# Layer 3's flow attention: flows in four column strips and kept as rows of nodes, queries and values scaled as rows, sums of keys times values folded with Wo

## The chip, the cores and the metric

One core of a Trainium2 chip. The metric is the device time of one execution of the whole program, in microseconds (us), as a median over runs. Everything is float32 unless a row says otherwise.

## The reference, cut to what matters

The program runs four layers of a graph network on 625 nodes with 512 features. The last layer's mixer is a "flow attention" with 8 heads of 64 features, and only that is changed:

```
q = sigmoid(x @ Wq + bq)   k = sigmoid(x @ Wk + bk)   v = x @ Wv + bv      # per head h: 625 x 64
sink_incoming    = 1 / ((q + EPS) . (k.sum(nodes) + EPS))
source_outgoing  = 1 / ((k + EPS) . (q.sum(nodes) + EPS))
conserved_sink   = (q + EPS) . ((k * source_outgoing).sum(nodes) + EPS)
conserved_source = clip((k + EPS) . ((q * sink_incoming).sum(nodes) + EPS), -1, 1)
sink_allocation    = sigmoid(conserved_sink)
source_competition = softmax(conserved_source over nodes) * 625
kv = k.T @ (v * source_competition)                                        # 64 x 64 per head
o  = (q * sink_incoming) @ kv * sink_allocation
x  = x + o @ Wo + bo
```

Beside it stands the layer's graph term, `agg @ weight.T`, which is added to the residual x. After it come a layer norm, a small GELU network, another norm and a ternary network.

## The kernel before, in words

`layer3` is one block. The order on each engine is written out by hand, and engines meet at semaphores. TensorE fills eight PSUM banks: four in turn for ScalarE (`for_act`, freed by `scalar_freed`) and four in turn for VectorE (`for_dve`, freed by `vector_freed`). An entry n waits until entry n-4 of the same four has been freed. `kept(name)` waits until ScalarE has taken the named entry. A product of float32 is written once in the code and stands in the trace as two MATMUL records, each as long as its number of moving columns; a transpose (`turned`) is one record.

Nodes come as 5 tiles of 125 rows (TILES, ROWS), features as 4 chunks of 128 (CH), and where nodes are columns, they are cut into halves of 313 and 312 (HALVES). The order before is:

1. Queries, then keys, as features by nodes (`T[0]`, `T[1]`, 128 x 4 x 625): 16 entries of four products for ScalarE, which applies the sigmoid and sums over nodes into `part`.
2. `size`, then the values as rows of nodes (`("v", t)`: 5 tiles, four products of 512 columns each). VectorE adds the bias (L4337), and rounds the ternary network's weights in `weights_rounded` (L4300 to L4302).
3. `flows(0)`: both incoming flows of all 8 heads, into 16 rows of PSUM, for two halves. Its stationary operand `wide` has 16 columns and its eight products a half are issued one after the other. VectorE keeps them as 16 x 625 (`keep_flows`) and takes the reciprocal (L4340).
4. `spreads(0, i, ...)` multiplies the 16 x 625 reciprocals by a 0/1 matrix, so that each head's row is copied to its 64 features; VectorE multiplies queries and keys by them and sums over nodes (L4344). Then `flows(1)` with the new sums.
5. ScalarE does sigmoid and exp on 16 x 625; `spreads(1, ...)` spreads both results, and VectorE scales queries (L4357) and keys (L4369) with them.
6. The scaled keys are transposed into rows (`("key", t)`, ScalarE keeps them in `z`), `shift` folds a bias, `("kv", p)` makes four 128 x 128 products over nodes, `("out", p, a)` multiplies queries by the two heads' diagonal blocks, and ScalarE keeps the result.
7. `("wo", t)`: 5 tiles, four products of 512 columns each, after which the norm begins.

The five products of the graph term (`graph(t)`) are placed between these. ScalarE keeps them in `G`, and one VectorE addition puts them into x (L4375).

Layer 2 of the same program already computes attention scores in four column strips (L2344) and gathers them into rows with a small 0/1 matrix (`a_gather`); this part is not changed.

Of the kernel before, what the change touches and what calls it, by code (L numbers as in the profile page):

```python
# [6 lines left out]
ALU = mybir.AluOpType  # L7
# [4 lines left out]
BF16 = mybir.dt.bfloat16  # L12
# [3851 lines left out]
def layer3(core, c, d, out):  # L3864
# [9 lines left out]
    with ExitStack() as ctx:  # L3874
# [15 lines left out]
        junk = sb("junk", [128, 2 * CH, 313], BF16)  # L3890
        wide = sb("wide", [128, 2, CH * HW])
        spread = sb("spread", [128, 2, CH, 128])
        flow_rows = sb("flow", [128, NODES])
        keep_rows = sb("keep", [128, NODES])
        flow, keep = flow_rows[0:HW, :], keep_rows[0:HW, :]
        offset = sb("offset", [HW, 2])
        es = sb("es", [HW, 1])
        kv = sb("kv", [128, CH, 128])
        part = sb("part", [128, 2, 2, CH, 2])
        total = sb("total", [128, 2, CH])  # L3900
# [12 lines left out]
        oT, x2T, r2, R, xq = xaT, aggT, V, z, G  # L3913
# [10 lines left out]
            "widened", "inverse_made", "flows_kept", "clipped", "exponents_done", "sink_made", "source_made",  # L3924
            "queries_scaled", "keys_scaled", "kv_made", "attended", "rows_rounded", "hidden_rounded", "tile_done",
            "stored", "gains_folded"]}
# [7 lines left out]
        with nc.Block() as block:  # L3934

            @block.gpsimd
            def _(gp):
                nc.gpsimd.memset(wide[:, :, :], 0.0)
                nc.gpsimd.memset(back[:, :], -ROUND)
                nc.gpsimd.memset(spread[:, :, :, :], 0.0)  # L3940
                nc.gpsimd.memset(flow_rows[:, :], 0.0)
                nc.gpsimd.memset(keep_rows[:, :], 0.0)
                for i in range(2):
                    nc.gpsimd.memset(T[i][:, :, NODES:NODES + 1], EPS)
                nc.gpsimd.memset(kv[:, :, :], 0.0).then_inc(sem["cleared"], 1)
                gp.wait_ge(sem["cleared"], 1)
                for i in range(2):
                    for p in range(CH):
                        for k in range(2):
                            row = HEADS * i + 2 * p + k  # L3950
                            last = nc.gpsimd.tensor_copy(spread[0:HW, i, p, HDIM * k:HDIM * (k + 1)],
                                                         c.ident[0:HW, row:row + 1].to_broadcast([HW, HDIM]))
                last.then_inc(sem["cleared"], 1)
# [8 lines left out]
            def _(pe):  # L3962
# [43 lines left out]

                def flows(n):

                    pe.wait_ge(sem["widened"], n + 1)
# [4 lines left out]
                def spreads(n, i, src):  # L4014
                    for p in range(CH):
                        for a, b in HALVES:
                            for_dve(("spread", n, i, p, a), [product(128, [(spread[:, i, p, :], src[:, a:b])], b - a)])

                def graph(t):
                    for_act(("graph", t), [product(ROWS, [(aggT[:, k, rows_of(t)], W["g"][:, k, :]) for k in range(CH)],  # L4020
                                                   DIM)])
# [18 lines left out]
                pe.wait_ge(sem["wv_landed"], 16)  # L4040
                for t in range(TILES):
                    for_dve(("v", t), [product(ROWS, [(xaT[:, k, rows_of(t)], W["v"][:, k, :]) for k in range(CH)], DIM)])
# [577 lines left out]
```

## Time and profile before

| | |
|---|---|
| median of 3 runs | 1624.69 us (1623.59 to 1641.59) |
| the profiled execution: own time | 1628.42 us |
| its span, first to last instruction | 1626.7 us |
| from the first `size` product to the first `wo` product | 1485.59 to 1568.97 us of the span |
| from there to the end | 57.73 us |
| mean granted TensorE clock | 0.974 |

The trace lists each instruction with its start and length. Lengths of matmuls include the time for the result to come out, so consecutive ones overlap: what a block of products takes is the distance from its start to the start of the next block. PE is TensorE's matmul unit, PEld its loading of the stationary operand, DVE VectorE, ACT ScalarE, POOL GpSimd.

### The profile page before, as it was taken

What the parts mean: (1) busy time and instruction counts of PE and PEld (TensorE: products, weight loads), DVE (VectorE), ACT (ScalarE), POOL (GpSimd) and SP (SyncE); (2) the same over time, 40 slices, a digit from 0 to 9 for tenths busy, and PEclk for the clock granted to TensorE, in tenths of its full rate; (3) what the DMA queues carried; (4) which work ended last, traced back from release to release, by engine and by line L of the source; (5) the groups of instructions that cost most, each with busy time, mean ns of one, the idle gap of its engine ahead of it and who ended that gap; (6) DMA issues with size and microseconds to landing.
All of it is one profiled execution on the core that took longest, in us unless ns stands there. A gap on an engine that the chain in (4) does not pass through costs nothing. (4 is left out here: it accounts for less than half of the span.)

```text
span 1626.7 us, 25993 instructions
## 1 busy us (share of the span) xinstructions
PE 1546.7 (95%) x9350; PEld 982.2 (60%) x9351; DVE 877.8 (54%) x2376; ACT 497.8 (31%) x1178; POOL 112.0 (7%) x194
## 2 busy tenths in 40 slices
PE   6999999999899989998999999999999999999995
PEld 3687644664456589995476754665544444465453
DVE  7676767873366675623634435643633343441457
ACT  2462244430120132321556314621122232221124
POOL 1010000000000003441000000000000000110000
PEclk9999999999899899998999999999899999999997
DMA  5340363100441188960200031304789999550001
GB/s 177 96 132 15 116 213 136 39 8 0 174 170 38 41 311 274 302 200 29 73 26 26 1 116 46 102 0 207 304 352 425 428 428 399 228 175 1 1 0 32
DMA packets 58548, 237.57 MB, mean 146 GB/s; under 512 B 13022, under 2 KB 16729, under 8 KB 49498
## 3 DMA queue, kind: packets, MB, share of 16 engines
q1 hardware_dynamic: 45076, 209.69, 34.4%
q0 software_dynamic: 13376, 26.60, 5.6%
q8 instruction: 61, 1.00, 0.2%
q14 instruction: 35, 0.29, 0.1%
HBM read 225.99 MB, written 10.24 MB: 145 GB/s over the span
## 5 line engine op out<-in xcount | busy, mean ns | idle before, releaser
L105 PE MATMUL psum<-ahead_arena 125*125 125x257 f32 (+2 forms) x720 | 215.8, 457 | 1.1 <-issue 0.7
L105 PEld LDWEIGHTS psum<-ahead_arena 125*125 125x125 f32 (+1 forms) x720 | 130.5, 188 | 76.5 <-issue 63.6
L3246 PE MATMUL psum<-ahead_arena,ahead_W 128*32 128x512 f32 x928 | 107.1, 601 | 1.8 <-DVE ahead_W L3768 1.0
L3225 PE MATMUL psum<-ahead_arena,ahead_W 128*32 128x256 f32 x1856 | 106.4, 381 | 2.1 <-DMA ahead_arena<-in_L_ffn_W 1.7
L105 PE MATMUL psum<-a_W,1_xn_turned 128*125 128x512 f32 x200 | 89.4, 596 | 1.2 <-DVE a_u L1577 1.2
L799 DVE TENSOR_SCALAR a0e_ring<-a0e_node,a0e_key 125x640 bf16<-125x640 f16 x216 | 69.1, 384 | 33.7 <-PE psum L607 31.8
L3225 PEld LDWEIGHTS psum<-ahead_arena,ahead_W 128*32 128x32 f32 x1856 | 57.7, 110 | 41.8 <-issue 5.5
L607 PEld LDWEIGHTS psum<-a0e_tables,a0e_ring 125*125 125x125 bf16 x1080 | 67.5, 138 | 11.5 <-issue 9.5
L607 PE MATMUL psum<-a0e_tables,a0e_ring 125*125 x1080 | 72.0, 223 | 1.8 <-issue 0.9
L105 PE MATMUL psum<-a_W,a0l_H 128*125 128x512 f32 x168 | 72.7, 593 | 0.7 <-issue 0.7
L105 PE MATMUL psum<-e_hT,e_W 128*128 128x156 f32 x512 | 70.9, 297 | 0.0
L3752 DVE TENSOR_TENSOR ahead_W<-psum,ahead_W 128x256 f32<-128x256 f32 x58 | 21.9, 419 | 88.6 <-PE psum L3234 88.6
L105 PE MATMUL psum<-e_xgT,e_W 128*128 128x156 f32 x512 | 69.2, 296 | 0.0
L105 PEld LDWEIGHTS psum<-e_hT,e_W 128*128 128x128 f32 x512 | 68.4, 190 | 0.0
L105 PEld LDWEIGHTS psum<-e_xgT,e_W 128*128 128x128 f32 x512 | 68.3, 190 | 0.0
L3246 PEld LDWEIGHTS psum<-ahead_arena,ahead_W 128*32 128x32 f32 x928 | 29.9, 111 | 62.3 <-issue 53.2
L105 PEld LDWEIGHTS psum<-a_W,1_xn_turned 128*125 128x125 f32 x200 | 36.5, 188 | 44.2 <-issue 43.4
L105 PEld LDWEIGHTS psum<-a_W,a0l_H 128*125 128x125 f32 x168 | 31.4, 188 | 40.7 <-issue 40.7
L105 PE MATMUL psum<-1_xn_turned,a_qkv 128*128 128x313 f32 (+1 forms) x176 | 49.3, 435 | 0.8 <-ACT 1_xn_turned L1096 0.8
L3434 ACT ACTIVATE ahead_W<-psum 128x512 f32<-128x512 f32 x29 | 17.4, 598 | 92.8 <-PE psum L3246 85.1
L105 PE MATMUL psum<-1_edges_from_to,1_xn_rows 125*128 125x313 f32 (+1 forms) x160 | 43.0, 426 | 1.3 <-PEq L3112 1.3
L2206 POOL DMA_INDIRECT e_got<-expert_rows,e_at_i x30 | 39.5, 1318 | 60.9 <-DMA expert_rows<-e_rows 53.5
(829 smaller groups left out, 2690.4 us busy)
## 6 DMA issues: line engine op xcount, KB each, us to landing
ahead_arena<-in_L_ffn_W SPq DMA_DIRECT2D x52, 2048.0 KB, 13.5
e_W<-in_L_ffn_W SPq DMA_DIRECT2D x16, 2048.0 KB
1_xn_turned<-half_shares SPq DMA_DIRECT2D x16, 256.0 KB, 8.2
a_stage<-in_L_gnn_W SPq DMA_DIRECT2D x8, 512.0 KB, 8.1
ahead_arena<-in_L_gnn_W SPq DMA_DIRECT2D x2, 2048.0 KB, 10.6
a_W<-in_L_gnn_W SPq DMA_DIRECT2D x3, 1024.0 KB, 5.5
a_qkv<-half_shares SPq DMA_DIRECT2D x11, 256.0 KB, 3.3
a_W<-in_L_ffn_w_down POOLq DMA_DIRECT2D x1, 2816.0 KB, 15.7
```

What stands on the lines that cost most here:

```text
L105: last = nc.tensor.matmul(bank[0:rows, at:at + cols], lhs, rhs, start=(n == 0), stop=(n == len(terms) - 1))
L607: last = nc.tensor.matmul(sums[k % 2][0:ROWS, 128 * s:128 * (s + 1)], ring[:, b, rows_of(s)], targets, start=False, stop=False, skip_group ...
L799: nc.vector.tensor_scalar(ring[:, b, :], node[:, :], key[:, k, b:b + STARTS][:, bass.ds(tile, 1)], None, ALU.is_equal).then_inc(made[b], QUAD)
L2206: nc.gpsimd.indirect_dma_start(out=got[:, e % 2, t, :], out_offset=None, in_=c.expert_rows[0:(e + 1) * TOP1, :], in_offset=bass.IndirectOf ...
L3225: last = nc.tensor.matmul(hid[a][g * SL:(g + 1) * SL, 0:HC], xgT[:, k, :], Wa[b][a][:, k, g, :], start=(k == 0), stop=(k == CH - 1))
L3246: last = nc.tensor.matmul(sums[g * SL:(g + 1) * SL, :], hT[:, a, m, g * SL:(g + 1) * SL], Wb[b][a][:, m, g, :], start=(a == 0 and m == 0), ...
L3434: nc.scalar.activation(part, sums[:, :], ACT.Copy).then_inc(sem["parts_kept"], 1)
L3752: nc.vector.tensor_tensor(hT[:, a, :, :].rearrange("p c (g n) -> p (c g) n", g=QT), turn[a][:, 0:HC].rearrange("p (f n) -> p f n", n=SL), ...
```

## The change

- **Flows in strips.** `wide` becomes [128, 8, 32]: one 32-column stationary operand for each of 4 chunks of keys' sums and of queries' sums. The eight products of a half go to four column strips of the array, each strip with its own chunk, and its own 32 rows of PSUM. The four strips are added when they are turned into rows: `gather` (128 x 16) has a one for each head in each strip, and `row_flows` multiplies each tile of `strips` by it, giving 125 x 16 for a tile of nodes.
- **Rows of nodes.** Sigmoid outputs are also transposed to rows, queries (`("rows", 0, t)`) between the key products, keys (`("rows", 1, t)`) after the first value tile. VectorE copies them (`keep_rows`). Reciprocals, sigmoid and exp are now taken on 125 x 5 x 16 or 125 x 5 x 8 elements.
- **Sums over nodes by TensorE.** `node_sums` multiplies the reciprocals (stationary, 32 columns) by the rows of queries and keys, in four strips; ScalarE copies the bank, `("sums")` turns it back to features, `widen` builds the new `wide`. No flow is spread over features any more.
- **Scaling rows.** VectorE multiplies the rows of queries by the product of sink_allocation and sink_incoming, and the rows of values by the exponentials, with a per-head factor that is broadcast over 64 features. The queries are transposed back (`("back", t)`), keys are not scaled at all. The softmax's sum comes from a product with ones (`norms`) and is folded into `kv`.
- **Folding with Wo.** `M = kv.T-block @ Wo` (four products of 512 columns) replaces `out`; `wo` multiplies the transposed queries by `M`.
- The graph products go to VectorE's banks, and VectorE adds each of them to x; `shift` and the folding of `W1` come earlier. `spread`, `junk`, `flow` and `keep` are gone; GpSimd fills `own_head`, `gather`, `gather_sums` and `inverse` at the start of the block instead.

The core of the diff (waits and declarations largely left out):

```diff
-                    for a, b in FLOW_HALVES:
-                        for_dve(("flow", n, a), [product(HW, [(wide[:, i, HW * p:HW * (p + 1)], T[i][:, p, a:b])
-                                                              for i in range(2) for p in range(CH)], b - a)])
+                    for a, b in FLOW_HALVES:
+                        m = for_vector.add(("flow", n, a))
+                        pe.wait_ge(sem["vector_freed"], m - 3)
+                        for i in range(2):
+                            for p in range(CH):
+                                last = nc.tensor.matmul(for_vector.bank(m)[STRIP * p:STRIP * (p + 1), 0:b - a],
+                                                        wide[:, CH * i + p, :], T[i][:, p, a:b], start=(i == 0),
+                                                        stop=(i == 1))
+                        last.then_inc(sem["vector_filled"], 1)
+                def row_flows(n):
+                    pe.wait_ge(sem["vector_freed"], for_vector.nth(("flow", n, FLOW_HALVES[1][0])))
+                    for_dve(("rows_flow", n), [product(ROWS, [(strips[:, rows_of(t)], gather[:, :])], HW, at=HW * t)
+                                               for t in range(TILES)])
+                def node_sums():
...
+                    for turn in range(3):
+                        for i in range(2):
+                            for part_, tiles in enumerate([(0, 1, 2), (3, 4)]):
+                                if turn < len(tiles):
+                                    at, t = STRIP * (2 * i + part_), tiles[turn]
+                                    last = nc.tensor.matmul(for_scalar.bank(n)[at:at + STRIP, 0:DIM], inverse[:, t, :],
+                                                            R[i][:, t, :], start=(turn == 0), stop=(turn == len(tiles) - 1))
...
+                        if i and m < CH - 1:
+                            kept(("q", CH - 1, HALVES[1][0]))
+                            turn_rows(0, range(2 * m, min(2 * m + 2, TILES)))
...
-                for t in range(TILES):
-                    for_dve(("v", t), ...)
-                flows(0)
-                graph(0)
-                graph(1)
-                pe.wait_ge(sem["inverse_made"], 1)
-                for i in range(2):
-                    spreads(0, i, flow_rows)
-                graph(2)
-                flows(1)
-                graph(3)
-                spreads(1, 0, keep_rows)
-                graph(4)
-                spreads(1, 1, flow_rows)
-                for t in range(TILES):
-                    for_act(("key", t), ...)
+                for_dve("shift", ...)
+                for_dve(("v", 0), [product(ROWS, values(0), DIM)])
+                kept(("k", CH - 1, HALVES[1][0]))
+                turn_rows(1, range(TILES))
+                pe.wait_ge(sem["widened"], 1)
+                flows(0)
+                for_dve(("v", 1), [product(ROWS, values(1), DIM)])
+                row_flows(0)
+                for_dve(("v", 2), [product(ROWS, values(2), DIM)])
+                pe.wait_ge(sem["inverse_made"], 1)
+                node_sums()
+                for_dve(("v", 3), [product(ROWS, values(3), DIM)])
+                kept("node_sums")
+                for_dve("sums", ...)
+                for_dve(("v", 4), [product(ROWS, values(4), DIM)])
+                pe.wait_ge(sem["widened"], 2)
+                flows(1)
+                for_dve(("graph", 0), [product(ROWS, graph(0), DIM)])
+                row_flows(1)
+                for_dve(("graph", 1), [product(ROWS, graph(1), DIM)])
+                for_dve(("graph", 2), [product(ROWS, graph(2), DIM)])
+                for t in range(TILES):
+                    pe.wait_ge(sem["queries_scaled"], t + 1)
+                    for_act(("back", t), ...)
+                for_dve("norms", ...)
+                pe.wait_ge(sem["values_scaled"], TILES)
                 for p in range(PAIRS):
-                    for_dve(("kv", p), [product(128, [(R[:, t, chunk(p)], V[:, t, chunk(p)]) for t in range(TILES)], 128)])
+                    for_dve(("kv", p), [product(128, [(V[:, t, chunk(p)], R[1][:, t, chunk(p)]) for t in range(TILES)], 128)])
+                for_dve(("graph", 3), [product(ROWS, graph(3), DIM)])
                 for p in range(PAIRS):
                     pe.wait_ge(sem["kv_made"], p + 1)
-                    for a, b in HALVES:
-                        for_act(("out", p, a), [product(128, [(kv[:, p, :], T[0][:, p, a:b])], b - a)])
+                    (for_act, for_dve)[p % 2](("M", p), [product(128, [(kv[:, p, :], W["o"][:, p, :])], DIM)])
+                for_dve(("graph", 4), [product(ROWS, graph(4), DIM)])
```

VectorE's new order around the first of its waits:

```diff
+                keep_rows(0)
                 kept(("k", CH - 1, HALVES[1][0]))
...
+                add_value(0)
+                keep_rows(1)
                 weights_rounded()
                 for k in range(CH):
                     last = nc.vector.tensor_scalar(W1[:, k, :], W1[:, k, :], gains[:, 2, k:k + 1], None, ALU.mult)
+                keep_strips(0)
+                add_value(1)
+                nc.vector.reciprocal(inverse[:, :, 0:HW], take(("rows_flow", 0))...)
```

## Rows read from the trace of the kernel before

**Rows 1.** The page, busy time of TensorE over the whole span.

```profile
PE 1546.7 (95%) x9350; PEld 982.2 (60%) x9351; DVE 877.8 (54%) x2376; ACT 497.8 (31%) x1178; POOL 112.0 (7%) x194
```

**Rows 2.** Busy us (instructions) of PE, PEld, DVE, ACT, POOL; granted clock; DMA.

```profile
1485.59:1568.97 83.38, 81.33 (x296) 43.56 (x294) 37.30 (x97) 12.34 (x25) 0.00 (x0) 1.00 0.00 0
1568.97:1626.70 57.73, 41.23 (x144) 23.02 (x144) 39.93 (x111) 21.22 (x38) 1.59 (x6) 0.80 0.07 23
```

**Rows 3.** Timeline of PE in the stage: start us, us, what, [idle before].

```profile
1485.73 17.41 PE L105 MATMUL psum<-a_Wv,a_xaT 128*125 128x512 f32 x40
1503.07 2.28 PE L105 MATMUL psum<-a_Tq,a_wide 128*16 128x313 f32 x8
...
1511.61 7.13 PE L105 MATMUL psum<-a_Wg,a_aggT 128*125 128x512 f32 x16
1518.57 8.60 PE L105 MATMUL psum<-a_flow,a_spread 128*128 128x313 f32 x32
1527.01 3.60 PE L105 MATMUL psum<-a_Wg,a_aggT 128*125 128x512 f32 x8
...
1542.60 4.38 PE L105 MATMUL psum<-a_keep,a_spread 128*128 128x313 f32 x16
1546.82 3.60 PE L105 MATMUL psum<-a_Wg,a_aggT 128*125 128x512 f32 x8
1550.25 4.38 PE L105 MATMUL psum<-a_flow,a_spread 128*128 128x313 f32 x16
1555.26 2.45 PE L102 MATMUL psum<-1_ident,a_Tk 128*125 128x128 f32 x20 [0.63 <-DVEq L4373]
1558.60 1.05 PE L105 MATMUL psum<-a_gains,a_W 128*128 128x1 f32 x8 [0.90 <-ACT a_z L4189]
1559.52 4.71 PE L105 MATMUL psum<-a_V,a_z 125*128 125x128 f32 x40
1564.07 4.38 PE L105 MATMUL psum<-a_Tq,a_kv 128*128 128x313 f32 x16
1568.97 17.43 PE L105 MATMUL psum<-a_Wo,a_xaT 128*125 128x512 f32 x40 [0.52 <-ACT a_xaT L4193]
```

**Rows 4.** Timeline of PE in layer 2, its scores in column strips.

```profile
973.70 2.31 PE L2344 MATMUL psum<-ahead_arena,ahead_wa 128*32 128x313 f32 x32
975.93 7.13 PE L105 MATMUL psum<-ahead_arena 128*125 128x512 f32 x16
982.90 1.16 PE L105 MATMUL psum<-a_gather,ahead_arena 128*125 128x8 f32 x10
```

**Rows 5.** Costliest groups of the page: four strips of 512 columns.

```profile
L3246 PE MATMUL psum<-ahead_arena,ahead_W 128*32 128x512 f32 x928 | 107.1, 601 | 1.8 <-DVE ahead_W L3768 1.0
```

**Rows 6.** Groups of DVE by form: busy us, mean ns, idle before.

```profile
L4337 DVE TENSOR_TENSOR a_V<-psum,a_Bv 125x512 f32<-125x512 f32 x5 | 3.5, 692 | 9.5 <-PE psum L105 9.4
L2713 DVE COPY ahead_arena<-psum 128x313 f32<-128x313 f32 x2 | 1.0, 482 | 17.2 <-PE psum L2344 17.2
L2786 DVE TENSOR_TENSOR ahead_arena<-psum,a_rd 125x256 f32<-125x256 f32 x10 | 4.2, 424 | 0.3
L4340 DVE RECIPROCAL a_flow<-a_flow 16x625 f32<-16x625 f32 x1 | 4.1, 4053 | 0.0
```

**Rows 7.** Timeline of DVE around the rounding of weights, and W1.

```profile
1487.69 0.49 DVE L4300 TENSOR_SCALAR a_qf<-1_xn_turned,a_scale 128x512 f32<-128x512 f32 x1
...
1490.98 0.69 DVE L4337 TENSOR_TENSOR a_V<-psum,a_Bv 125x512 f32<-125x512 f32 x1
...
1559.95 0.88 DVE L4378 TENSOR_SCALAR a_W<-a_W,a_gains 128x128 f32<-128x128 f32 x4
```

**Rows 8.** Timeline of ACT: the table of exp is loaded.

```profile
1541.75 1.28 ACT L4184 ACT_TABLE_LOAD   x1
```

**Rows 9.** An idle TensorE and the granted clock after it, layer 2.

```profile
1169.17 0.27 PE L3259 MATMUL psum<-ahead_W,r_cols 20*1 20x64 f32 x2 [2.20 <-DVE ahead_W L3719]
...
1170.00:1175.00 5.00, 5.00 (x24) 3.46 (x20) 2.70 (x15) 0.21 (x1) 0.00 (x0) 0.66 1.03 436
```

More of the change, by code:

```diff
@@ L3889, in layer3 @@
         V = sb("V", [ROWS, TILES, DIM])
[L3890 to L3897, printed above, removed]
+        Rq = sb("Rq", [ROWS, TILES, DIM])
+        own_head = sb("own_head", [128, CH, HEADS])
+        gather = sb("gather", [128, HW])
+        gather_sums = sb("gather_sums", [128, 2, HEADS])
+        wide = sb("wide", [128, HEADS, STRIP])
+        strips = sb("strips", [128, NODES])
+        offset = sb("offset", [128, 1])
+        inverse = sb("inverse", [ROWS, TILES, STRIP])
+        sink = sb("sink", [ROWS, TILES, HEADS])
+        source = sb("source", [ROWS, TILES, HEADS])
+        norms = sb("norms", [128, HEADS])
         kv = sb("kv", [128, CH, 128])
-        part = sb("part", [128, 2, 2, CH, 2])
-        total = sb("total", [128, 2, CH])
+        part = sb("part", [128, 2, CH, 2])
+        total = sb("total", [128, HEADS])
         hT = sb("hT", [FF3, NODES])
@@ L4005, in first_queries, with turn_rows, values, graph @@
                     last.then_inc(sem["scalar_filled"], 1)
+                def turn_rows(i, tiles):
+                    for t in tiles:
+                        for_dve(("rows", i, t), [turned(ROWS, 128, T[i][:, m, rows_of(t)], c.ident[:, :], at=128 * m)
+                                                 for m in range(CH)])
+                def values(t):
+                    return [(xaT[:, k, rows_of(t)], W["v"][:, k, :]) for k in range(CH)]
+                def graph(t):
+                    return [(aggT[:, k, rows_of(t)], W["g"][:, k, :]) for k in range(CH)]
@@ new lines, in _ @@
+                flows(1)
[5 more added lines that the diff above has]
+                    pe.wait_ge(sem["queries_scaled"], t + 1)
+                    for_act(("back", t), [turned(128, ROWS, Rq[:, t, chunk(m)], c.ident[0:ROWS, 0:ROWS], at=128 * m)
+                                          for m in range(CH)])
@@ new lines, in add_graph, with keep_rows, by_head @@
+                def add_graph(t):
+                    nc.vector.tensor_tensor(c.x[:, t, :], c.x[:, t, :], take(("graph", t))[0:ROWS, :], ALU.add).then_inc(
+                        sem["vector_freed"], 1)
+                def keep_rows(i):
+                    for t in range(TILES):
+                        nc.vector.tensor_copy(R[i][:, t, :], take(("rows", i, t))[0:ROWS, :]).then_inc(
+                            sem["vector_freed"], 1)
+                def by_head(rows):
+                    return rows.rearrange("p (h e) -> p h e", h=HEADS)
@@ new lines, in _ @@
+                dve.wait_ge(sem["exponents_done"], 1)
+                for t in range(TILES):
+                    nc.vector.tensor_tensor(by_head(V[:, t, :]), by_head(V[:, t, :]),
+                                            source[:, t, :].unsqueeze(2).to_broadcast([ROWS, HEADS, HDIM]),
+                                            ALU.mult).then_inc(sem["values_scaled"], 1)
+                add_graph(1)
+                add_graph(2)
+                step(nc.vector.reciprocal(norms[:, :], take("norms")[:, 0:HEADS]))
```

218 lines of the change are left out of this document (102 added, 116 removed).

## The prediction

> **What bounds the kernel now.** I read the page first: TensorE is busy for 95% of the span, VectorE for 54%, ScalarE for 31% [rows 1]. That is an average over seven stages, so the second view is the table of windows for the stage that is changed. From the first `size` product to the first `wo` product there are 83.38 us, of which TensorE is busy for 81.33, VectorE for 37.30 and ScalarE for 12.34, at a granted clock of 1.00 (2.4 GHz) [rows 2]. The third view, the timeline of PE alone, says the same in detail: each block starts where the one before it ends, and only three waits stand in it, of 0.63, 0.90 and 0.52 us [rows 3]. So this stage is as long as its list of products, and a change is worth the difference of the two lists, as long as the other engines can follow. After `wo` begins nothing is changed in kind (57.73 us [rows 2]), and before the key products neither.
>
> **What is removed.** Block lengths are distances between starts [rows 3]. One `flows` takes 1503.07 to 1511.61 = 8.54 us (four blocks of that form), and there are two of them: 17.08. The spreads take 1518.57 to 1527.01 = 8.44, 1542.60 to 1546.82 = 4.22, and 1550.25 to 1555.26 = 5.01 with the wait for the last scaled keys: 17.67. The key transposes with the wait for ScalarE's last copy take 1555.26 to 1558.60 = 3.34. `out` with its wait for ScalarE takes 1564.07 to 1568.97 = 4.90. Sum removed: 17.08 + 17.67 + 3.34 + 4.90 = 42.99 us. What stays on the path with the same work is `size` and `shift` (about 1.1), the values, the graph products and `kv` (4.55): 83.38 - 42.99 = 40.39.
>
> **What is added, on TensorE.**
> - Flows in strips. Layer 2 has 32 records of the very form, 32 columns stationary and 313 moving, and they take 973.70 to 975.93 = 2.23 us [rows 4]. Each new `flows` also has 2 halves x 8 products x 2 records = 32. Two of them: 4.46.
> - `row_flows`: 10 records with 125 stationary columns and few moving ones. The like of it in layer 2 takes (1.16 - 0.25) / 9 = 0.10 us a record [rows 4], where 0.25 is the length of one record. Two times 10: 2.0.
> - Transposes: 20 for queries' rows, 20 for keys' rows, 20 back. The key transposes of before are 20 in 2.45 us, less the 0.28 in which the last result comes out, so 0.114 each [rows 3]. Three times 2.3 = 6.9. The first 20 lie between the key products, and TensorE is fully busy there too, so they cost their whole length.
> - `node_sums`: 3 turns x 2 records of 512 columns, four strips side by side (two in the last turn). A record of that form costs 107.1 / 928 = 0.115 us when four share the array [rows 5], so a group of four 0.46; six groups 2.7.
> - `sums` and `norms`: 8 and 10 small records with 128 stationary columns, at the 0.92 us of the eight of `shift` (1558.60 to 1559.52) [rows 3]: 0.9 + 1.15 = 2.1.
> - `M`: 8 records of 512 columns. 40 such take 17.34 us (1485.73 to 1503.07) [rows 3]: 3.5.
>
> Sum: 4.46 + 2.0 + 6.9 + 2.7 + 2.1 + 3.5 = 21.7 us. Without any wait the change is worth 42.99 - 21.7 = 21.3 us.
>
> The Trainium skill ("TensorEngine Tiling (Array Packing)", Key Properties) says that a change of the tiling mode drains TensorE, and the new list has six such changes where the old had none. The block of strips in layer 2 bears it in part: its 2.23 us stand against 8 groups of 313 columns at the 0.264 us of a full-width record (2.11), so at most 0.12 us went to getting in, and that is in my price [rows 4]. By the rule a drain would cost up to the 0.16 us by which a record outlasts its columns, an estimate worked out from that page's rule and the rows, 1.0 us for all six; the sum would then be 20.3 instead of 21.3.
>
> **Where TensorE will wait.** I go through the hand-written order and ask at each wait which engine is late.
> - `row_flows(0)` waits for `keep_strips(0)` on VectorE, and in front of that are queued: the bias of value tile 0, five copies of keys' rows, the rounding of weights, the folding of W1. Counted from the end of `("v", 0)` on TensorE: 0.3 us for the result to arrive, 0.72 for the addition, 5 x 0.70 for copies of 125 x 512 from PSUM (0.692 for the addition of that size; the 128 x 313 copy at 0.482 is on the same line per element [rows 6]), 1487.69 to 1490.98 = 3.3 for the rounding, 0.9 for W1 [rows 7], and 1.2 for the three operations that keep the strips (the 0.482 twice, and a small one). That is 9.9 us. TensorE has meanwhile 2.3 (transposes) + 2.23 (flows) + 3.43 (value tile 1) = 8.0. So TensorE waits for **1.9 us**. It might be 0.9 if the plain copies run at 0.5, and it can't be below 0, because the work in front is never negative.
> - `node_sums` waits for the reciprocal on 125 x 80. L4340 took 4.05 us for 625 elements a partition [rows 6], so 80 take some 0.6; value tile 2 (3.43) covers it.
> - `flows(1)` waits for `widen`, covered by value tile 4; `row_flows(1)` waits for the second strips (1.2), covered by graph tile 0.
> - `back` and `kv` wait for the longest new chain: clip 0.25, sigmoid 0.25, one small multiplication 0.2, five multiplications of query rows, five of value rows. The exp's table load of 1.28 us [rows 8] runs on ScalarE beside the query rows. The multiplications have a factor broadcast over 64 features; L2786 is of that kind and takes 0.424 for 256 elements against 0.692 for 512 plain ones [rows 6], so I take 0.72 each: 7.9 us for the chain. Before `kv` TensorE has two graph tiles (6.9), `back` (2.3) and `norms` (1.15): 10.3. The cover is 2.4 us thick. If each multiplication took twice as long, the chain would end at 15.1, and TensorE would wait 4.8 us.
> - After `kv`, graph tile 3 covers the diagonal blocks, graph tile 4 covers the copies of `M`. Here the three old waits (0.63 + 0.90 + 0.52, all inside the blocks removed) get no successor.
> - ScalarE loses the five copies into `G` and eight of `out`, and gains five of `back`, two of `M` and one of the sums; with 12.34 us busy of 83 [rows 2] it is nowhere late. GpSimd's new fillings end some 45 us before VectorE asks for them. No DMA is moved; `wo_landed` was due long before.
>
> The sum: 42.99 - 21.7 - 1.9 = **19.4 us**. On the profiled execution (span 1626.7, own time 1628.42) that gives a span of 1607.3 and a time of 1609.0; its own time lies 3.7 above the median of the runs, so on the median 1624.7 - 19.4 = **1605.3**. That is 1.2% less, and since about 2% is what a measurement of this kernel can tell from no change, it falls within "the same".
>
> **The rivals.**
> - *VectorE becomes the bound.* For it: it does ten new row copies and ten row multiplications, and at `row_flows(0)` it is already the late one. Against it: in all it has, by the prices above, some 31 us of work in the 61.7 that remain. The price is the thin cover above: a chain 2.4 us longer starts to cost, and slow broadcasts would give 1605 + 5 = **1610**. The Trainium skill ("TensorEngine Tiling (Array Packing)", PSUM Bottleneck) says that once strips have sped TensorE up, emptying PSUM may become the bound and that both ScalarE and VectorE should do it. The rows agree at one place, the 1.9 us above; here all row copies are VectorE's while ScalarE idles.
> - *The clock falls at the new wait.* In layer 2 TensorE once stood idle for 2.20 us, then did about 1 us of tiny products, and the clock was at 1.2 GHz for part of the next 5 us (0.66 granted) [rows 9]. `row_flows(0)` is just that: 1.9 us idle, then 1.0 us of 16-column products. The stage of before had no fall with waits up to 0.90 us [rows 2, 3]. One fall of that kind is (1.00 - 0.66) x 5 / 0.5 = 3.4 us at half speed, 1.7 us lost: **1607**, inside the range. *Slower than before* would be the same mechanism held: if from `row_flows(0)` to the first `wo` the small products kept the clock at 1.2 GHz, the 47 us of work there (61.7 less `size`, `shift`, two value tiles, transposes, one `flows` and the wait, 14.3 in all) would cost 47 more, for 1605 + 47 = **1652**. It decides from 19.4 us of TensorE work done at the lower clock. Against it: the 40 short records of `kv` and 28 around them ran at 1.00 before, and long products lie between the new short ones.
> - *The strips don't run side by side here,* because each has its own moving chunk. Then 64 records of 0.264 (16.9) stand for 4.46, and 20 of 0.43 (8.6) for 2.7: 18.3 back, and **1623**: the change doesn't do what it says. Against it: the strips of layer 2 also take a chunk each [rows 4].
> - *VectorE is quicker than priced:* no wait at `row_flows(0)`, **1603**.
>
> **How the numbers follow.** My forecast (1602 to 1607, with or without one fall of the clock) 0.75; VectorE late at `kv` or elsewhere (1607 to 1613) 0.15; strips not side by side (1613 to 1623) 0.03; the clock held low (over 1624) 0.03; something better than priced, such as a shorter tail, 0.04. The range of 1598 to 1613 takes in 0.9 of these by their mechanisms and leaves room for the spread of the runs (1623.59 to 1641.59 before). Faster by over 2% means below 1592.2, which none of the terms reaches: 0.02. Slower by over 2% means above 1657, held clock and more: 0.01. The rest, 0.97, lies within 2%.
>
> **What the changed kernel's profile would show.** The distance from the first `size` product to the first `wo` product is 83.38 us before and should be 83.38 - 19.4 - 2.3 = 61.7, since 2.3 of what is added lies ahead of it, among the key products. The blocks of `wide` with 32 columns should take 2.2 us each, `node_sums` 2.7, and the blocks of products with `spread` are gone. PE's largest idle time in the stage should stand before the first products with `gather`, about 1.9 us and released by VectorE's strips; `kv` should start without a wait. If the strips take 8 us, the third rival is right; if an idle time of several us stands before the products of `V` and `z`, the first; a granted clock below 1.00 between `row_flows(0)` and `wo` shows the second. What would make the forecast wrong is a cost that the list of products doesn't contain, above all a VectorE operation far from its price.

## The result, and the profile after

| | before | after |
|---|---|---|
| median of 15 runs | 1627.36 us (1623.59 to 1645.02) | 1605.85 us (1599.98 to 1622.2) |
| the profiled execution: own time | 1628.42 us | 1622.2 us |
| its span | 1626.7 us | 1620.5 us |
| first `size` product to first `wo` product | 83.38 us | 60.86 us |
| from there to the end | 57.73 us | 57.80 us |
| mean granted TensorE clock | 0.974 | 0.964 |

The ratio is 0.9871, with a 95% interval of 0.9847 to 0.9896: 16.9 to 24.9 us less. A second series of the same two kernels (e11) gave 1618.35 against 1626.09 us, ratio 0.993 (0.9896 to 0.9965). The stage is alike in both, 60.86 and 60.87 us; what differs is how many runs have a mean clock of at most 0.966, two of 15 and six of 12. The profiled execution of the changed kernel is one of those that take some 15 us longer than most, because of the clock in layer 1, far ahead of the change (last section). So positions in the span are not compared here, but distances between blocks of the stage.

The page, busy time of each engine, after. TensorE has 4.6 us less work than in [rows 1], although its granted clock was low for 36 of its products in layer 1.

```profile
PE 1542.1 (95%) x9376; PEld 979.1 (60%) x9377; DVE 871.2 (54%) x2347; ACT 492.7 (30%) x1167; POOL 108.7 (7%) x184
```

The windows after, columns as in [rows 2]: from the first key product to `size`, the stage, and the tail.

```profile
1482.82:1501.84 19.02, 19.02 (x85) 14.29 (x84) 3.27 (x5) 4.90 (x16) 0.00 (x0) 1.00 0.00 1
1501.84:1562.70 60.86, 59.93 (x301) 33.14 (x300) 27.14 (x62) 8.12 (x15) 0.00 (x0) 1.00 0.00 1
1562.70:1620.50 57.80, 41.14 (x145) 22.97 (x143) 40.59 (x112) 19.79 (x36) 1.60 (x6) 0.80 0.07 23
```

The tail is unchanged, so the gain is all in the first two rows. Key products to `size` took 1468.76 to 1485.59 = 16.83 before and take 19.02 now, 2.19 more for the 20 transposes of queries' rows; from the first key product to `wo` it was 100.21 and is 79.88, **20.33 us less**. In the stage TensorE is idle for 60.86 - 59.93 = 0.93 us, at full clock.

The timeline of PE in the stage after, as in [rows 3]:

```profile
1506.39 2.35 PE L102 MATMUL psum<-1_ident,a_Tk 128*125 128x128 f32 x20
1508.69 0.73 PE L4035 MATMUL psum<-a_Tq,a_wide 128*32 128x313 f32 x8
...
1510.93 3.70 PE L105 MATMUL psum<-a_Wv,a_xaT 128*125 128x512 f32 x8
1515.56 1.26 PE L105 MATMUL psum<-a_gather,a_strips 128*125 128x16 f32 x10 [0.93 <-DVE a_strips L4316]
1516.67 3.68 PE L105 MATMUL psum<-a_Wv,a_xaT 128*125 128x512 f32 x8
1520.28 0.62 PE L4055 MATMUL psum<-a_Rq,a_inverse 125*32 125x512 f32 x2
...
1522.99 3.70 PE L105 MATMUL psum<-a_Wv,a_xaT 128*125 128x512 f32 x8
1526.52 0.96 PE L105 MATMUL psum<-a_gather_sums,a_Wk 128*128 128x16 f32 x8
1527.33 3.68 PE L105 MATMUL psum<-a_Wv,a_xaT 128*125 128x512 f32 x8
1530.94 0.73 PE L4035 MATMUL psum<-a_Tq,a_wide 128*32 128x313 f32 x8
...
1533.18 3.70 PE L105 MATMUL psum<-a_Wg,a_aggT 128*125 128x512 f32 x8
...
1544.68 2.30 PE L102 MATMUL psum<-1_ident,a_Rq 125*128 125x125 f32 x20
1546.81 1.18 PE L105 MATMUL psum<-a_source,1_ones 125*128 125x8 f32 x10
1547.85 4.71 PE L105 MATMUL psum<-a_z,a_V 125*128 125x128 f32 x40
1552.40 3.60 PE L105 MATMUL psum<-a_Wg,a_aggT 128*125 128x512 f32 x8
1555.84 3.60 PE L105 MATMUL psum<-a_Wo,a_kv 128*128 128x512 f32 x8
1559.27 3.60 PE L105 MATMUL psum<-a_Wg,a_aggT 128*125 128x512 f32 x8
```

`flows(0)` takes 1508.69 to 1510.93 = 2.24 us where it took 8.54, `flows(1)` 1530.94 to 1533.18 = 2.24, `node_sums` 1520.28 to 1522.99 = 2.71. One wait is left, 0.93 us at `row_flows(0)`, and VectorE's strips end it. Nothing stands before `kv` (1547.85).

The timeline of DVE after, around that wait:

```profile
1506.66 0.69 DVE L4320 TENSOR_TENSOR a_V<-psum,a_Bv 125x512 f32<-125x512 f32 x1 [3.35 <-PE psum L105]
1507.27 3.07 DVE L4329 COPY a_z<-psum 125x512 f32<-125x512 f32 x5
1510.26 0.47 DVE L4343 TENSOR_SCALAR a_qf<-1_xn_turned,a_scale 128x512 f32<-128x512 f32 x1
...
1513.54 0.88 DVE L4389 TENSOR_SCALAR a_W<-a_W,a_gains 128x128 f32<-128x128 f32 x4
1514.33 0.15 DVE L4313 COPY a_offset<-psum 128x1 f32<-128x1 f32 x1
1514.51 0.55 DVE L4314 TENSOR_SCALAR a_strips<-psum,a_offset 128x313 f32<-128x313 f32 x1
1514.97 0.53 DVE L4316 TENSOR_SCALAR a_strips<-psum,a_offset 128x312 f32<-128x312 f32 x1
```

From the addition of value tile 0 to the kept strips VectorE never stands still: copies of rows 3.0 us, rounding 3.3 (1510.26 to 1513.54), W1 0.8, strips 1.2.

### The profile page after: what moved, and what is told of

Its sections match the earlier page's. It is cut to its first block and busy times, and to the rows that moved or that the text cites. A ratio compares the mean times of both kernels' runs of the same rounds, so it can differ in the third digit from the quotient of the medians.

```text
span 1620.5 us, 26010 instructions
## 1 busy us (share of the span) xinstructions
PE 1542.1 (95%) x9376; PEld 979.1 (60%) x9377; DVE 871.2 (54%) x2347; ACT 492.7 (30%) x1167; POOL 108.7 (7%) x184
## 5 line engine op out<-in xcount | busy, mean ns | idle before, releaser
L105 PE MATMUL psum<-a_Wkv,1_xn_turned 128*125 128x512 f32 x80 | 37.5, 632 | 6.7 <-DMA a_Wkv<-in_L_mix_Wkv 6.7
```

Of the source, the lines that this page charges most:

```text
L105: last = nc.tensor.matmul(bank[0:rows, at:at + cols], lhs, rhs, start=(n == 0), stop=(n == len(terms) - 1))
```

## The experiments

The theory: the stage is as long as TensorE's list of products plus the waits in it, VectorE is late only at `row_flows(0)`, and the gain is the difference of the two lists. The rivals: the strips save nothing, VectorE is late at `kv`, the clock falls at the new waits. "Stage" is the time from the first `size` product to the first `wo` product in the profiled execution.

**e1: flows in one strip.** The changed kernel, with all eight products of a half in one strip of 32 columns.

```diff
-   ...bank(m)[STRIP * p:STRIP * (p + 1), 0:b - a], wide[:, CH * i + p, :], ..., start=(i == 0), stop=(i == 1))
+   ...bank(m)[0:STRIP, 0:b - a], wide[:, CH * i + p, :], ..., start=(i + p == 0), stop=(i + p == CH))
```

> The changed kernel, but all eight products of a half go to the same column strip (rows 0 to 31 of the bank), one after the other; rows of nodes are taken from that strip alone. If the gain of the flows comes from four strips side by side, each flows block takes 32 x 0.264 = 8.5 us instead of 2.2, the first wait before row_flows(0) (0.93) vanishes under the longer block, and the stage from the first size product to the first wo product is 60.9 + 2 x 6.3 - 0.9 = 72.5 us: about 1617. If it comes from the narrower stationary operand or anything but the strips, the stage stays at 61 to 62 us.

Measured: 1621.01 us, ratio 0.9965 (0.9931 to 0.9999), stage 72.83, without a wait at `row_flows(0)`. The stage is as expected; the median lies 4 us over the 1617, with two of the eight runs at a mean clock of 0.964. The timeline of PE in e1, where in the changed kernel 0.53 us separate such groups:

```profile
1510.21 2.27 PE L4035 MATMUL psum<-a_Tq,a_wide 128*32 128x313 f32 x8
1512.31 2.27 PE L4035 MATMUL psum<-a_Tk,a_wide 128*32 128x313 f32 x8
```

The same 32 records take 2.11 us by eight here (8.52 a `flows`) and 0.53 by eight in four strips. So the strips do run side by side, and those of the flows are worth about 12 of the 20.33 us: more than half of the change. The missing wait shows the other side: with each `flows` 6.3 us shorter, VectorE's queue has 6.3 us less cover.

**e2: before, with the strips alone.** Flows in four strips, added by a product with `gather` after VectorE has copied them; spreads, key transposes and `out` as before.

```diff
+   m = for_vector.add(("strip", n, a))          # eight products into four strips
+   nc.vector.tensor_copy(strips[:, a:b], take(("strip", n, a))[:, 0:b - a])
+   for_dve(("flow", n, a), [product(HW, [(gather[:, :], strips[:, a:b])], b - a)])
```

> The kernel before with one part alone: its flows in four strips (2.2 us instead of 8.5 each), which VectorE copies and TensorE adds up into 16 rows with four records of 313 columns (1.1 us); spreads, key transposes and out stay. If gains are differences of TensorE's list, the stage shrinks by 17.1 - 4.5 - 2.1 = 10.5 less the waits that this order opens: the chain strips, 16-row flows, reciprocal (5.6 us) has one graph product (3.4) as its cover, so 2.2 us, and some 1 us elsewhere. Stage 83.4 - 10.5 + 3 = 76 us, and 7 us less in all. If the flows only pay together with the rest, because the reciprocal on 16 partitions then lies open, the stage stays above 81.

Measured: 1621.7 us, ratio 0.9969 (0.9934 to 1.0004), stage 78.97, so 4.4 us saved in place of the 7.4 expected. The timeline of PE in e2:

```profile
1527.84 8.70 PE L105 MATMUL psum<-a_flow,a_spread 128*128 128x313 f32 x32 [1.78 <-DVE a_flow L4367]
1556.35 4.48 PE L105 MATMUL psum<-a_flow,a_spread 128*128 128x313 f32 x16 [1.51 <-DVE a_flow L4393]
1565.73 6.34 PE L105 MATMUL psum<-a_V,a_z 125*128 125x128 f32 x40
```

The two shorter `flows` save 12.6 and the two collecting products cost 2.3, but then TensorE waits 1.78 and 1.51 us for VectorE, and `kv` takes 6.2 us instead of 4.55, with a granted clock of 0.72 in it: 4.9 us in all. The last 0.9 is in the graph and spread blocks, which end up to 0.26 us later ahead of a wait or of a block of another shape. The strips alone hand a quarter of their gain to waits. These come from the detour, not from the shorter `flows`: `flows(0)`, copy, collecting product, 16-row flows and reciprocal (4.05 us) follow each other, and of the two graph tiles that covered the reciprocal before, one now lies ahead of the collecting product. At the second wait too, a graph tile has moved ahead of it, and what is late there is the scaling behind the exp (L4393 of e2). The changed kernel takes the reciprocals on 125 partitions (0.66 us for 125 x 80, against 4.05 in [rows 6]), one value tile covers them, and its stage has no wait there.

**e3: the rounding later.** In the changed kernel, `weights_rounded` and the folding of W1 go behind the first reciprocal, out of the way of the strips.

```diff
-                weights_rounded()
-                (fold W1)
                 keep_strips(0)
                 add_value(1)
                 (reciprocal of the rows)
                 add_value(2)
+                weights_rounded()
+                (fold W1)
```

> The changed kernel, with the rounding of weights and the folding of W1 moved behind the reciprocal and value tile 2, where VectorE idles 5.6 us. If the 0.93 us wait before row_flows(0) is VectorE's queue in front of keep_strips(0), it vanishes, nothing else moves, and the stage is 60.9 - 0.9 = 60.0 us. If the strips wait for something else (the copies, a bank), part of the wait stays.

**e7: the copies by ScalarE.** ScalarE copies the five tiles of keys' rows, VectorE keeps its order.

```diff
-                keep_rows(1)
+                for t in range(TILES):
+                    nc.scalar.activation(R[1][:, t, :], take(("rows", 1, t))[0:ROWS, :], ACT.Copy)
```

> The changed kernel with the five copies of keys' rows given to ScalarE, which idles there. VectorE's queue before keep_strips(0) is 3.1 us shorter, so if that queue is the wait, the 0.93 us vanish and the stage is 60.0 us, as with the later rounding; the two don't add up. If the wait has another cause it stays at 60.9.

Measured: stages of 59.67 (one execution of 1601.93 us) and 59.65 (1607.29 us), neither with a wait. The windows of the stage in e3, then in e7:

```profile
1482.88:1542.55 59.67, 59.67 (x302) 33.23 (x301) 27.33 (x62) 8.12 (x15) 0.00 (x0) 1.00 0.00 1
```

```profile
1488.32:1547.97 59.65, 59.65 (x302) 33.03 (x301) 24.24 (x57) 10.68 (x20) 0.00 (x0) 1.00 0.00 1
```

PE's busy time equals the stage in both. Two unlike ways to free VectorE give the same 1.2 us, so VectorE's queue made the wait. That is 0.3 more than the 0.93 of the wait: without it value tile 1 takes 3.54 us instead of 3.70, and `row_flows(0)` 1.01 instead of 1.11.

**e5 and e6: a longer wait.** Two, then five additions of 125 x 512 (some 0.6 us each) ahead of the strips.

```diff
+                for t in range(2):        # e6: range(5)
+                    nc.vector.tensor_tensor(G[:, t, :], c.x[:, t, :], c.x[:, t, :], ALU.add)
                 keep_strips(0)
```

> The changed kernel with two more additions of 125 x 512 (into an unused tile) in front of keep_strips(0): TensorE's wait before row_flows(0) grows from 0.93 by 2 x 0.61 to 2.15 us. By VectorE's queue alone the stage is 60.9 + 1.2 = 62.1 us at a clock of 1.00. If a wait of this size makes the clock fall, as behind the 2.20 us in layer 2, the granted clock after row_flows(0) is 0.5 for some 3.4 us and the stage is 63.8.

> The same with five more additions: the wait grows to 4.0 us. Without a fall of the clock the stage is 60.9 + 3.05 = 64.0 us; with one fall of 3.4 us at half speed 65.7; if the short products keep it low, far more (each us of work at 1.2 GHz costs one).

Measured: waits of 2.13 and 3.94 us, stages of 63.77 and 66.51 (one execution each, 1624.53 and 1615.31 us; that of e5 has the low clock of layer 1). So the clock fell in both: 63.8 and 65.7 were expected for one fall, 62.1 and 64.0 for none. The timeline of PE in e5, and the window behind the wait:

```profile
1516.43 1.26 PE L105 MATMUL psum<-a_gather,a_strips 128*125 128x16 f32 x10 [2.13 <-DVE a_strips L4316]
1517.54 5.37 PE L105 MATMUL psum<-a_Wv,a_xaT 128*125 128x512 f32 x8
```

```profile
1518.00:1522.00 4.00, 4.00 (x7) 1.62 (x6) 0.39 (x1) 0.00 (x0) 0.00 (x0) 0.57 0.00 0
```

The timeline of PE in e6:

```profile
1506.09 2.28 PE L105 MATMUL psum<-a_gather,a_strips 128*125 128x16 f32 x10 [3.94 <-DVE a_strips L4316]
1508.21 5.31 PE L105 MATMUL psum<-a_Wv,a_xaT 128*125 128x512 f32 x8
```

The stage of e5 is 2.91 longer than that of the changed kernel: 1.20 of wait, and 1.67 in the value tile behind it (5.37 against 3.70), with a granted clock of 0.57 in the 4 us shown. In e6 the wait is 3.01 longer, and the clock is already low in the `gather` products (2.28 against 1.26), so the fall costs 1.0 + 1.6 = 2.6. A fall costs 1.7 to 2.6 us here and ends within one value tile: from there to the first `wo` product the granted clock is 1.00 in both.

**e4: each multiplication twice.** Query and value rows are each multiplied twice, so the chain before `kv` is 6.1 us longer.

```diff
+                    nc.vector.tensor_tensor(by_head(G[:, t, :]), by_head(Rq[:, t, :]), sink[...].to_broadcast(...), ALU.mult)
...
+                    nc.vector.tensor_tensor(by_head(G[:, t, :]), by_head(V[:, t, :]), source[...].to_broadcast(...), ALU.mult)
```

> The changed kernel with every per-head multiplication of query rows and value rows done twice (the first result goes to an unused tile): VectorE's chain before kv grows by 10 x 0.61 = 6.1 us. In the changed kernel value rows are ready at 1544.80 and kv starts at 1547.85, so the cover is 3.05 us. If the cover is what I read, TensorE waits 6.1 - 3.05 = 3.0 us before kv, and the stage is 63.9 us. If VectorE is not near the path there, less; if the graph additions or the banks behind them are late as well, more.

Measured: 1609.24 us (one execution), stage 68.37 where 63.9 was expected. The timeline of PE in e4:

```profile
1495.13 1.26 PE L105 MATMUL psum<-a_gather,a_strips 128*125 128x16 f32 x10 [0.93 <-DVE a_strips L4316]
1496.24 5.37 PE L105 MATMUL psum<-a_Wv,a_xaT 128*125 128x512 f32 x8
...
1532.34 7.31 PE L105 MATMUL psum<-a_z,a_V 125*128 125x128 f32 x40 [3.07 <-DVE a_V L4426]
```

The wait before `kv` is 3.07 us, as expected (3.0): in the changed kernel the value rows are scaled 3.05 us ahead of need. Of the 4.5 us missing, 4.3 are two falls of the clock: `kv` takes 7.14 us instead of 4.55 (2.6), and the value tile behind `row_flows(0)` 5.37 instead of 3.70 (1.7). The fall at the value tile follows the same wait of 0.93 us at which the clock stayed at 1.00 in the profiles of the changed kernel and of e11. The length of the wait doesn't decide it by itself.

**e8: `out` instead of `M`.** `kv` is multiplied with the queries and then with Wo, as before the change.

```diff
-                    (for_act, for_dve)[p % 2](("M", p), [product(128, [(kv[:, p, :], W["o"][:, p, :])], DIM)])
+                    for_act(("out", p, a), [product(128, [(kv[:, p, :], T[0][:, p, a:b])], b - a)])
```

> The changed kernel with the folding of Wo undone: 16 records of 313 columns (out) instead of 8 of 512 (M), wo reads their copy and Wo itself. By the list of products out is 4.2 and M 3.4, so the stage is 60.9 + 0.8 = 61.7 us, since graph tile 4 still covers ScalarE's last copy. If the folding hid more than that (ScalarE's eight copies in the path), the stage is over 63.

Measured: stage 61.65, as expected; folding with Wo is worth 0.8 us. (The one execution took 1622.27 us, again with the low clock in layer 1.)

**e9: one product for the norms.** e3, and in addition one product of 40 columns in place of five of 8, summed by VectorE.

```diff
-                for_dve("norms", [product(128, [(c.ones[0:ROWS, :], source[:, t, :]) for t in range(TILES)], HEADS)])
+                for_dve("norms", [product(128, [(c.ones[0:ROWS, :], source as 125 x 40)], TILES * HEADS)])
```

> The changed kernel with the later rounding, and with the five norms products (10 records of 8 columns, 1.04 us) made one product of 40 columns (2 records), summed over tiles by VectorE in a place where it waits anyway. By TensorE's list the stage is 59.7 - 0.8 = 58.9 us against 60.9 of the changed kernel: 2.0 us less. If the later steps have no slack, the kv products wait or the first copy of kv is late by the 0.3 us of the new reduction, and the stage stays above 59.3.

Measured: stage 58.77, 2.1 us below the changed kernel's. The runs give 1605.99 us, ratio 0.9882 (0.9824 to 0.9941); with one of the five at 1622.28 us, they can't be told from those of the changed kernel.

**e10: e9, and 125 rows in place of 78 in layer 1.** The profiles of the changed kernel, e1, e2, e5 and e8, have a low clock during 36 of the 40 products at the end of layer 1 (L1834, L1840), which contract over 78 rows. Here they contract over 125, 47 of them zero.

```diff
-        rows = sb("rows", [TOPC, 2, 2, DIM])
+        rows = sb("rows", [ROWS, 2, 2, DIM])      # filled with zeros first
-        nc.tensor.matmul(..., places[last_expert][0:TOPC, i, rows_of(t)], ...)
+        nc.tensor.matmul(..., places[last_expert][0:ROWS, i, rows_of(t)], ...)
```

> The last one, with the second part of layer 1's expert sums (L1834, L1840) contracted over 125 rows of which 47 are zeros, instead of 78 rows. It tests what parts the executions into some near 1603 and some near 1620: in the traces these 40 products take 17 us in some executions and 34 us at 0.50 clock in others, after the same wait of about 1.9 us. If the few rows keep the clock from coming back, the clock comes back within some 4 us of the wait in every execution, and no run is above 1610. If the wait alone decides, the runs stay in two heaps, with and without 14 us more.

**e11: the changed kernel again,** beside e9 and e10.

> The changed kernel once more, on the same chip and in the same rounds as the two before it, for a direct comparison: stage 60.9 us, wait 0.93 us before row_flows(0), 2 us above the version with the later rounding and one norms product; two heaps of runs, 14 us apart.

Measured: e10 1602.55 us (1600.71 to 1607.1), ratio 0.9856 (0.9815 to 0.9898); e11 1618.35 us (1605.29 to 1623.99), ratio 0.993 (0.9896 to 0.9965). Of the twelve executions of e11, six had a mean clock of at most 0.966 and took 1621.71 to 1623.99; none of e10's five did. As expected, no run of e10 is above 1610. But the clock did not fall in its profile at all (wait 1.00 us, granted clock 1.00 behind it), so that profile doesn't show how 125 rows end a fall.

**e12: the same 125 rows behind a longer wait.** e10, with six additions ahead of the bias for which TensorE waits before these products.

```diff
+                        if e == last_expert and k == CH - 1:
+                            for f in range(6):
+                                nc.vector.tensor_tensor(W2[0:ROWS, 0, f, :], c.xn[:, f % TILES, :], c.xn[:, f % TILES, :], ALU.add)
```

> The 40 products of layer 1's end with their 47 zero rows, as in the run before, with six additions of 125 x 512 by VectorE put ahead of the last bias that TensorE waits for there, so that its wait grows from 1.0 to 1.9 us by about 3.7 us and the clock should be low at its end in every run. If the 125 contracted rows bring the clock back within the next few microseconds after any wait, all runs lie together at 1602.5 + 3.7 + about 2 lost to one fall, 1608 us, and none 14 us above. If the wait alone decides whether the clock stays low for all 40 products, a part of the runs, as of the changed kernel, or all of them lie near 1608 + 14 = 1622 us, with a mean clock near 0.96.

Measured: 1604.5 us (1600.56 to 1610.39), ratio 0.9857 (0.9823 to 0.989); 1608 was expected. The wait grew to 1.86 us only, not to five: VectorE reached the bias 2.0 us later than in e10 (744.08 against 742.08), and TensorE came to its wait 1.1 later as well. The 1.86 is just the wait of the changed kernel's profile, so the two can be laid side by side. The timeline of PE at the end of layer 1, in the kernel before:

```profile
743.42 1.77 PE L102 MATMUL psum<-1_ident,e_oT 128*78 128x128 f32 x8 [1.90 <-DVE e_oT L2135]
744.98 2.91 PE L1834 MATMUL psum<-e_rows,e_got 78*125 78x512 f32 x4
747.73 3.60 PE L1840 MATMUL psum<-e_rows,e_others 78*125 78x512 f32 x8
```

In the changed kernel:

```profile
743.60 1.58 PE L102 MATMUL psum<-1_ident,e_oT 128*78 128x128 f32 x8 [1.87 <-DVE e_oT L2135]
744.98 3.62 PE L1834 MATMUL psum<-e_rows,e_got 78*125 78x512 f32 x4
748.39 7.04 PE L1840 MATMUL psum<-e_rows,e_others 78*125 78x512 f32 x8
```

In e12:

```profile
744.51 1.07 PE L102 MATMUL psum<-1_ident,e_oT 128*78 128x128 f32 x8 [1.86 <-DVE e_oT L2139]
745.41 1.88 PE L1834 MATMUL psum<-e_rows,e_got 125*125 125x512 f32 x4
747.13 3.60 PE L1840 MATMUL psum<-e_rows,e_others 125*125 125x512 f32 x8
```

The first line of each decides how these are to be read. In e12 the eight transposes right behind the wait take 0.90 us from start to start (744.51 to 745.41), as in e10 and in every profile without a fall: the clock did not fall. In the kernel before (1.56) and in the changed one (1.38) it had fallen before any product over 78 rows began. In the kernel before it was back after three or four of them (2.75 us for the first four, in place of 1.72), in the changed one it stayed low for all 36. So the condition of this experiment, a low clock at the end of the wait, was not met in its profile, and whether 125 rows end a fall sooner than 78 is not shown. Nothing of this code differs between before and changed.

## Why the prediction was right

The forecast was 1605.3 us and the median 1605.85; key products to `wo` got 20.33 us shorter, where 19.4 were forecast. The second number is the test of the mechanism. That the first is met so closely is partly luck: the kernel before came out at 1627.36 instead of the 1624.69 that the forecast starts from, and in the second series (e11), where six of twelve runs had such a low mean clock, the same changed kernel had a median of 1618.35, outside the range of 1598 to 1613. The prediction has no term for that. By its own steps:

- **The bound.** Right: TensorE is busy for 59.93 of the stage's 60.86 us, and e1, e3, e8 and e9 came out within 0.4 us of what the list of products gave.
- **Removed, 42.99.** These were read as distances in the profile and are gone; 40.39 were to stay. What stays takes 40.9: several value and graph tiles now take 0.09 to 0.17 more where a block of another shape follows, and value tile 1 takes 0.26 more ahead of the wait (value tile 2, 1516.67 to 1520.28 = 3.61, against 1552.40 to 1555.84 = 3.44 for a graph tile with its like behind it). I had given the new blocks no such cost.
- **Added, 21.7.** Measured 21.2: `flows` 4.48 (4.46 predicted), `row_flows` 1.11 and 1.01 (2.0), transposes 2.19, 2.30 and 2.13 (6.9), `node_sums` 2.71 (2.7), sums and norms 0.81 and 1.04 (2.1), `M` 3.43 (3.5). Every price came from a block of the same or a like form elsewhere in the trace.
- **The rule on tiling modes** (the Trainium skill, "TensorEngine Tiling (Array Packing)", Key Properties: a change of mode drains TensorE) was weighed at 1.0 us. Distances between starts hold any drain there is. The blocks of strips take what they took in layer 2 (2.24 against 2.23), and the three entries into strips cost 0.17 each: 3.61 for value tiles 2 and 4 against 3.44, and 2.30 for the transposes ahead of `flows(0)` against 2.13. That is 0.5 us in all and not 1.0. Most of it isn't special to strips: the five value tiles of before, 17.34 us [rows 3], are 0.14 more than five times 3.44, and they led into `flows` of 16 columns in one strip. Whether those 16 columns were themselves another mode, no run shows.
- **The wait at `row_flows(0)`: the term that was mis-sized.** 1.9 forecast, 0.93 measured, with the right place and releaser. Five copies cost 3.0 us (0.60 from start to start), not 3.5, and VectorE's chain from the end of value tile 0 took 9.1 (1506.39 to 1515.50), not 9.9; TensorE's cover took 8.2, not 8.0. The prediction's "0.9 if the plain copies run at 0.5" is met by luck: they ran at 0.60, which gives half of that 1.0 us, and the rest is 0.1 each from the addition and W1, and 0.2 from the longer cover. That "the wait is VectorE's queue" e3 and e7 showed. The Trainium skill (the same page, PSUM Bottleneck) would have both ScalarE and VectorE empty PSUM; e7 did so at one place and gained 1.2 us in the stage, as e3 did without it.
- **The chain before `kv`.** Cover of 2.4 forecast, 3.05 measured (the value rows are done at 1544.80, `kv` starts at 1547.85), and e4 bears it out with a wait of 3.07 for a chain 6.1 longer: the multiplications with a broadcast factor took 0.62 each, not 0.72. The rival of slow broadcasts is ruled out.
- **Strips not side by side** (1623): ruled out. e1 is this rival built for the flows, and its stage is 12 us longer. For `node_sums` the 2.71 us of its 20 records say the same, which one after the other would take 8.6 by the prediction's price.
- **The clock.** The mechanism of "one fall, 1.7 us lost" is real: e4 and e5 each show a fall at `row_flows(0)` of just 1.67. In the two profiles of the changed kernel it did not occur at 0.93 us of wait, in e4 it did at the same wait. "Held low from `row_flows(0)` to `wo`" was in no profile of the changed stage: even after 3.94 us of wait the clock was back behind one value tile. I had this risk in the wrong place: where the clock stayed low in the changed kernel's profile was the end of layer 1, which the change doesn't touch.
- **The tail,** 57.80 against 57.73, as said.

## What to carry to other kernels

Where one engine is busy for over 97% of a stage, as here, price the stage as a list: each block from a block of the same form anywhere in the trace, start to start; here six such prices summed to 21.7 us, and 21.2 were measured. Spend the care on the places where another engine must follow, and build that engine's queue operation by operation: a `flows` that shrinks by 6.3 us also takes away 6.3 us in which others worked (with the long one, in e1, the wait of 0.93 us is gone), and a detour over VectorE that stands alone hands part of the gain to waits (3.3 us in e2). A gain of 2 us in a stage (e9) can't be seen in the median while another stage has a clock that moves 15 us; fix or measure that one first.

## What the runs showed of the hardware that was not expected

**A low clock can last for 31 us of products without a pause.** At the end of layer 1 TensorE waits for VectorE, makes eight transposes, and then does 36 products of 512 columns over 78 rows without a gap. In the profiled executions:

| products over | wait before the transposes | transposes, start to start | granted clock 5 to 15 us after their start | kernels |
|---|---|---|---|---|
| 78 rows | 1.87, 1.90, 3.06, 1.53, 1.45 us | 1.29 to 1.73 us | 0.50 | changed, e1, e2, e5, e8 |
| 78 rows | 1.90, 1.98 us | 1.56, 1.70 us | 1.00 (low for the first 3 to 4 us) | before, e7 |
| 78 rows | none, 1.03, 1.22, 1.24, 1.28 us | 0.88 to 0.91 us | 1.00 | e4, e3, e6, e9, e11 |
| 125 rows | 1.00, 1.86 us | 0.90 us | 1.00 | e10, e12 |

In the first two rows the clock fell behind the wait, in the last two it did not. At 0.50 the 36 products take 30.9 us, where they take 15.6 in e10. That is about the distance between the two groups in which the runs of these kernels lie: 8 of 27 runs of the changed kernel (with e11) had a mean clock of at most 0.967, 2 of 8 of e1 and 1 of 5 of e9, but none of the 11 with 125 rows. In the stage of layer 3 a fall lasted some 3.2 to 5.2 us (twice the time lost), in products over 125 or 128 rows.

**What the 78 rows have to do with it is not shown.** No profile has a fall at this place together with 125 rows, so none shows that 125 rows bring the clock back sooner. For them speak the 11 runs; if the two series of the changed kernel are pooled, chance alone gives 11 such runs in about one case of 22. Against them speaks that e10's wait was the shortest of all but e4's none, and that behind waits of up to 1.28 us the clock did not fall over 78 rows either. In e12, at 1.86 us, the clock did not fall in the one profile, and its six runs are few. What would settle it are more profiles with 125 rows behind a wait of 2 to 3 us. Why two of the seven falls over 78 rows ended early, and why 8 of 27 runs of the changed kernel show a low mean clock against 7 of 61 of the kernel before (two of them told by their time alone, 1641.59 and 1645.02 us), stays open too.

**The best version.** e10 and e12 have the smallest medians, 1602.55 and 1604.5 us, and ratios of 0.9856 and 0.9857 to the kernel before. Their intervals overlap that of the change (0.9847 to 0.9896), so that they beat it is likely from the stage (58.77 against 60.86 us) and not shown by the medians. Whether the group of long runs is missing for good, 11 runs can't say.

**A factor broadcast along the row costs nothing here.** The timeline of DVE in the changed kernel, the rows of queries and of values with their factor per head, broadcast over 64 features:

```profile
1538.69 3.10 DVE L4416 TENSOR_TENSOR a_Rq<-a_Rq,a_sink 125x512 f32<-125x512 f32 x5
1541.71 3.09 DVE L4421 TENSOR_TENSOR a_V<-a_V,a_source 125x512 f32<-125x512 f32 x5
```

Five multiplications take 3.1 us, as do five additions of the same size without a broadcast operand in e6:

```profile
1501.84 3.09 DVE L4392 TENSOR_TENSOR a_G<-1_x_rows 125x512 f32<-125x512 f32 x5
```
